# First rows of a two-layer retention block loaded tile by tile, normalised on VectorE, and transposed into two banks

## What is computed

```python
# the first stage: x = x + _L0_attn_a_ref(_layernorm(x, axis=-1), ...), where X is the argument
for i in range(L):
    Xn = _layernorm(X, ln1_w[i], ln1_b[i])
    Q = jnp.einsum('bsd,hdk->bhsk', Xn, WQ[i])
    K = jnp.einsum('bsd,hdk->bhsk', Xn, WK[i])
    V = jnp.einsum('bsd,hdk->bhsk', Xn, WV[i])
    Q = Q * cosq + _rotate_every_two(Q) * sinq
    K = K * cosk + _rotate_every_two(K) * sink
    scores = jnp.einsum('bhsk,bhtk->bhst', Q, K) * Dm[None]
    Yh = jnp.einsum('bhst,bhtk->bhsk', scores, V)
    Y = _groupnorm(Yh.transpose(0, 2, 1, 3).reshape(B, S, H * HD), gn_w[i], gn_b[i])
    G = jax.nn.silu(Xn @ WG[i])
    Y = G * Y @ WO[i] + X
    Yn = _layernorm(Y, ln2_w[i], ln2_b[i])
    X = jax.nn.silu(Yn @ ffn_w1[i] + ffn_b1[i]) @ ffn_w2[i] + ffn_b2[i] + Y
```

## Time and profile before

| | us |
|---|---|
| median of 3 runs | 1516.62 |
| lowest and highest | 1515.74, 1516.77 |
| the profiled execution | 1518.72 |
| its span, first to last instruction | 1516.9 |

### The profile page before, as it was taken

The page is one execution under the profiler, slowest core; times in us unless marked ns, Lnnn a source line. Parts: engine busy times, 40 slices in busy tenths (PEclk is TensorE's granted clock), DMA queues, the critical chain, the costliest instruction groups (busy, mean ns, idle before and its releaser), DMA issues. The chain is left out here.

```text
span 1516.9 us, 36350 instructions
## 1 busy us (share of the span) xinstructions
PE 1443.2 (95%) x13066; PEld 1196.5 (79%) x13066; DVE 1046.7 (69%) x2272; ACT 936.7 (62%) x1760; POOL 809.2 (53%) x843
## 2 busy tenths in 40 slices
PE   4999999899998999999999999997999999989998
PEld 3777777799996788887899988886777777768886
DVE  4777877565446887785755668775777777756775
ACT  5556555465554545545655567775777777757775
POOL 2566676312013666663523257775666666636674
PEclk9999999999999999999999999999999999999999
DMA  7000000100001000000300010000000000000011
GB/s 247 2 2 2 0 2 2 35 1 1 1 1 56 2 2 0 1 2 1 125 29 15 1 40 1 0 1 2 2 1 0 0 0 0 0 2 1 31 41 42
DMA packets 21095, 26.27 MB, mean 17 GB/s; under 512 B 1904, under 2 KB 19056, under 8 KB 20848
## 3 DMA queue, kind: packets, MB, share of 16 engines
q1 hardware_dynamic: 18432, 21.64, 4.3%
q10 hardware_dynamic: 2544, 3.04, 0.6%
HBM read 20.48 MB, written 4.19 MB: 16 GB/s over the span
## 5 line engine op out<-in xcount | busy, mean ns | idle before, releaser
L543 DVE TENSOR_TENSOR ffn_h_lo<-ffn_h,ffn_h_hi 128x512 fp32r<-128x512 f32 x112 | 94.0, 841 | 116.1 <-ACT ffn_h_hi L750 116.0
L749 ACT ACTIVATE ffn_h<-ffn_hp,c_b 128x512 f32<-128x512 f32 x112 | 77.2, 689 | 153.2 <-PE ffn_hp L846 152.7
L543 DVE TENSOR_TENSOR ternary_ffn_h_lo<-ternary_ffn_h,ternary_ffn_h_hi 128x512 fp32r<-128x512 f32 x128 | 110.0, 860 | 75.0 <-ACT ternary_ffn_h_hi L750 74.8
L1187 POOL TENSOR_TENSOR ret_qk<-ret_qk,ret_qk_sin 128x512 f32<-128x512 f32 x64 | 82.6, 1291 | 103.2 <-DVE ret_qk_sin L1284 102.7
L857 PE MATMUL ternary_ffn_yp<-down_ternary,ternary_ffn_h_hi 128*128 128x256 f32 x512 | 132.6, 291 | 0.0
L857 PE MATMUL ffn_yp<-down_hi,ffn_h_hi 128*128 128x256 f32 x448 | 127.7, 285 | 0.9 <-DVE ffn_h_lo L543 0.9
L857 PE MATMUL ternary_ffn_yp<-down_ternary,ternary_ffn_h_lo 128*128 128x256 f32 x512 | 127.6, 281 | 0.0
L1193 POOL TENSOR_TENSOR ret_rstd<-ret_sums,ret_minus_half 128x16 f32<-128x16 f32 x32 | 103.7, 3240 | 42.9 <-DVE ret_sums L1326 42.9
L857 PE MATMUL ffn_yp<-down_hi,ffn_h_lo 128*128 128x256 f32 x448 | 125.2, 279 | 0.0
L857 PE MATMUL ffn_yp<-down_lo,ffn_h_hi 128*128 128x256 f32 x448 | 125.2, 279 | 0.0
L2081 POOL TENSOR_TENSOR win_rms<-win_rms,win_minus_half 128x20 f32<-128x20 f32 x31 | 115.2, 3716 | 2.6
(11 more groups left out here) (315 smaller groups left out, 4786.5 us busy)
## 6 DMA issues: line engine op xcount, KB each, us to landing
X<-in_x SPq DMA_DIRECT2D x8, 512.0 KB, 10.1
staging<-in_w SPq DMA_DIRECT2D x4, 1024.0 KB, 8.5
ffn_x_in<-in_x SPq DMA_DIRECT2D x8, 512.0 KB, 3.9
out<-X SPq DMA_DIRECT2D x7, 512.0 KB, 2.9
rotary<-in_rotary ACTq DMA_DIRECT2D x1, 1024.0 KB, 7.6
staging<-in_w_up SPq DMA_DIRECT2D x1, 1024.0 KB, 4.9
staging<-in_w_down SPq DMA_DIRECT2D x1, 1024.0 KB, 7.5
staging<-in_wqkv ACTq DMA_DIRECT2D x1, 768.0 KB, 5.9
```

Source lines behind the costliest of these rows:

```text
L543: nc.vector.tensor_tensor(h_lo[:, m % R, :], h[:, m % R, :], h_hi[:, m % R, :].bitcast(F32), ALU.subtract).then_inc(h_ready, 1)
L749: nc.scalar.activation(h[:, m % R, :], hp[m % 2][:, :], fn, bias=bias)
L1187: nc.gpsimd.tensor_tensor(qk[:, r, :, :, :], qk[:, r, :, :, :], qk_sin[:, r, :, :, :], ALU.add).then_inc(qk_done, 1)
```

## The change

- SyncE loads block 0 as four tiles of 128 KB, each with its own semaphore; blocks 2 to 7 wait until the tables of ScalarE's queue have landed.
- ScalarE issues ident and ln1 first, loads its activation table, waits for tile 0, and then issues wqkv, rotary and decay, wg and wo, and the other tables.
- VectorE waits for each tile's rows by itself. For blocks 0 and 1 GpSimd makes the scale of the projections alone (`first_scale`), and VectorE normalises the rows with it (`first_normalise`); the scale of the rows in place is made later (`scale_in_place`), and ScalarE writes the rows of block 1 in place in step 2 of body 1.
- The second half of block 0 is transposed into tr[0], without a wait for the first.
- The low half of wv (2) comes after the first input_low, that of the gate (3) and the statistics of block 1 at the end of body 0, that of the output (4) behind first_normalise(1) in body 1. SyncE's wait for all five low halves ahead of in_w stays as it is.

The core of the diff (the waits, the order and the new functions; left out are the declarations of semaphores and unchanged lines around):

```diff
--- before.py
+++ after.py
+        def transposed(b, j):
+            return tr[0] if first is not None and at_start(b) and j == 1 else tr[1]
...
         @block.sync
         def _(sp):
             if first is not None:
-                for b in range(NB):
+                for t in range(TB):
+                    sp.dma_start(X[:, t, :], first["x"][P * t:P * (t + 1), :]).then_inc(tile_loaded[t], 16)
+                for b in range(1, NB):
                     at = b // 2 + CPB * (b % 2)
                     if b == 1:
                         sp.wait_ge(qkv_loaded, 16)
+                    if b == 2:
+                        sp.wait_ge(tables_loaded, 16 * (len(first["tables"]) - 2))
                     sp.dma_start(X[:, TB * at:TB * (at + 1), :],
                                  first["x"][BT * at:BT * (at + 1), :].rearrange("(t p) d -> p t d", p=P)
                                  ).then_inc(x_loaded[b], 16)
...
+            def first_scale(b):
+
+                pool.wait_ge(mv_done, b + 1)
+                apart(pool, pool_waited)
+                nc.gpsimd.tensor_scalar(work[:, 0, 0, :], mv[:, b, :, 1], 1.0 + EPS, EPS * EPS, ALU.mult, ALU.add
+                                        ).then_inc(eps_added, 1)
+                pool.wait_ge(eps_added, 2 * b + 1)
+                nc.gpsimd.tensor_tensor(scale[:, b, 0, 0, :], work[:, 0, 0, :], minus_half[:, 0:TB], ALU.pow
+                                        ).then_inc(first_scaled, 1)
+
+            def scale_in_place(b):
+
+                apart(pool, pool_waited)
+                nc.gpsimd.tensor_scalar(work[:, 0, 1, :], mv[:, b, :, 1], EPS, None, ALU.add).then_inc(eps_added, 1)
+                pool.wait_ge(eps_added, 2 * b + 2)
+                nc.gpsimd.tensor_tensor(scale[:, b, 0, 1, :], work[:, 0, 1, :], minus_half[:, 0:TB], ALU.pow
+                                        ).then_inc(scale_work, 1)
+                pool.wait_ge(scale_work, 2 * b + 1)
+                nc.gpsimd.tensor_tensor(work[:, 1, 1, :], mv[:, b, :, 0], scale[:, b, 0, 1, :], ALU.mult
+                                        ).then_inc(scale_work, 1)
+                pool.wait_ge(scale_work, 2 * b + 2)
+                apart(pool, pool_waited)
+                nc.gpsimd.tensor_scalar(scale[:, b, 1, 1, :], work[:, 1, 1, :], -1.0, None, ALU.mult
+                                        ).then_inc(scale_done, 1)
...
                     if k % TB == TB - 1 and fresh(2 * i + k // TB):
-                        scales(2 * i + k // TB, k // TB)
+                        if first is not None and at_start(i):
+                            first_scale(k // TB)
+                            if k == TB - 1:
+                                scale_in_place(0)
+                        else:
+                            scales(2 * i + k // TB, k // TB)
+                    if first is not None and at_start(n):
+                        scale_in_place(1)
...
+            def x_wait(b, at, t):
+
+                if at_start(b):
+                    dve.wait_ge(tile_loaded[t], 16)
+                elif isinstance(b, int):
...
+                if first is not None and not last_block(b) and not after_last(b) and (t == 0 or at_start(b)):
+                    x_wait(b, at, t)
...
+            def first_normalise(b):
+
+                dve.wait_ge(first_scaled, b + 1)
+                if b == 1:
+                    dve.wait_ge(tp_full, KD)
+                for t in range(TB):
+                    last = nc.vector.tensor_scalar(xn[:, t, :], X[:, CPB * TB * b + t, :], mv[:, b, t, 0:1],
+                                                   scale[:, b, 0, 0, t:t + 1],
+                                                   ALU.subtract, ALU.mult)
+                last.then_inc(xn_done, 1)
...
                     if first is not None and at_start(n):
-                        dve.wait_ge(tables_loaded, 16 * len(first["tables"]))
+                        dve.wait_ge(rotary_loaded, 16 * 2)
                     if live(n, NT):
                         rotate(n, i, k - AHEAD)
+                    if first is not None and at_start(n - 1):
+                        dve.wait_ge(tables_loaded, 16 * (len(first["tables"]) - 2))
                     if live(n - 1, NT):
                         masked(n - 1, k - 1)
                     if live(n, NT):
                         values(n, k)
+                    if first is not None and at_start(n):
+                        first_normalise(1)
+                        own_low(4)
...
+                        if first is not None and at_start(i) and k == TB + 1:
+                            own_low(2)
+                        if first is not None and at_start(i) and k == U - 1:
+                            own_low(3)
+                            for t in range(TB):
+                                statistics(1, 0, 1, t)
+                            aggregate(1, 1)
...
+                    if first is not None and at_start(i) and k >= TB:
+                        pass
+                    elif fresh(2 * i + k // TB) or (after_last(2 * i + k // TB) and i == N):
...
                     if at_start(i) and k == TB - 2:
                         if first is not None:
+                            first_normalise(0)
                             centre_values()
-                            for j in range(3):
+                            for j in range(2):
                                 own_low(j)
                         dve.wait_ge(consts_set, 3)
-                    if at_start(i) and k == TB and first is not None:
-                        for j in range(3, len(first["halves"])):
-                            own_low(j)
...
+                    last = nc.scalar.activation(out, transposed(b, j)[:, :], ACT.Identity,
...
+                        if t == 0 and fresh(b + 1) and not (first is not None and isinstance(b, int) and b < 1):
                             normalise(b + 1, i, at + 1)
-                            if first is not None and at_start(b + 1):
-                                act.wait_ge(weights_loaded, 16 * (len(first["weights"]) - 1))
-                                for j in range(3, len(first["halves"])):
-                                    own_high(j)
-                            elif first is not None and not last_block(b + 1):
+                            if first is not None and not last_block(b + 1):
                                 rows_in_place(b + 1, i, at + 1)
+                        if t == 2 and first is not None and at_start(b):
+                            act.wait_ge(scale_done, 2)
+                            rows_in_place(1, i, at + 1)
                         if live(n, NT):
                             gates(b, t // 2, at)
...
+                        if first is not None and at_start(i) and k == TB + 1:
+                            act.wait_ge(early_loaded, 16 * len(first["early"]))
                         if fresh(b + 1):
                             inputs(b + 1, t // 2, at + 1)
+                        if first is not None and at_start(i) and k == TB + 1:
+                            act.wait_ge(v_centred, 1)
+                            own_high(2)
+                        if first is not None and at_start(i) and k == U - 1:
+                            act.wait_ge(weights_loaded, 16 * (len(first["weights"]) - 1))
+                            for j in range(3, len(first["halves"])):
+                                own_high(j)
...
                         act.wait_ge(qkv_loaded, 16)
                         own_high(0)
                         own_high(1)
-                        act.wait_ge(v_centred, 1)
-                        own_high(2)
                     if at_start(i) and k == U - 1 and first is not None:
+                        act.wait_ge(scale_done, 1)
                         rows_in_place(0, i, 0)
-                        act.wait_ge(tables_loaded, 16 * len(first["tables"]))
+                        act.wait_ge(tables_loaded, 16 * (len(first["tables"]) - 2))
                     if isinstance(i, int) and i == 1 and k < len(halves):
...
             if first is not None:
+                prefetch(act, first["early"], early_loaded)
+                act.wait_ge(consts_set, 1)
+                nc.scalar.activation(table_set[:, :], minus_half[:, 0:1], ACT.Silu)
+                act.wait_ge(tile_loaded[0], 16)
                 prefetch(act, first["weights"][0:1], qkv_loaded)
-                prefetch(act, first["early"], early_loaded)
+                prefetch(act, first["tables"][0:2], rotary_loaded)
                 prefetch(act, first["weights"][1:], weights_loaded)
-                prefetch(act, first["tables"], tables_loaded)
-                act.wait_ge(early_loaded, 16 * len(first["early"]))
-                nc.scalar.activation(table_set[:, :], ident[:, 0:1], ACT.Silu)
+                prefetch(act, first["tables"][2:], tables_loaded)
...
                 if at_start(g) and first is not None:
```

(40 more changed lines are left out.)

## The result

The changed kernel is slower: 1521.38 us against 1516.78 for the one before (medians of 18 runs each), a ratio of 1.0031 with a 95% interval of 1.0025 to 1.0038, or about 4.7 us. The forecast was 1519.9, 3.3 us slower. The profiled execution has a span of 1518.9 us against 1516.9; single executions spread over 5.0 us before and 6.9 after, so the span's 2.0 us say less than the ratio, and what follows is read at points of the first 60 us.

The account below looks back on a forecast made before the run. The start was taken as bound by transferred bytes, with in_w's landing ending the last wait. The 5.1 us won are spent waiting and in_w lands 3.3 us later: median 1516.62 plus 3.3 is 1519.9 us, range 1514.5 to 1522.8.

Parts of the forecast that it names:

- What bounds the start: First 50 us: bytes bound the start, in_w landing at 29.3 behind 9.33 MB; the work chain ahead has slack.
- Start: Block 0 up to the first projection: it comes at 16.0 instead of 21.14, 5.1 us earlier.
- What moves behind it: VectorE and GpSimd work behind the first projection: own_low(4) ends at 22.9, releasing SyncE's in_w issue, before at 16.77.
- Transfers: Start-up loads: same bytes but engines stand empty at times, so in_w lands at 32.6 instead of 29.3, +3.3 us.
- the time of 1517.4 at the higher rate: Time if the last 5.24 MB of loads passed at the fabric's 435 GB/s, in 12.0 us.
- the forecast's own floor from in_w's issue: in_w alone, issued at 22.9, lands no earlier than 31.3, +2.0 us.
- A rule weighed in the forecast: Transfers from any engine share the same 16 DMA engines, so reordering can't shorten the load phase.
- Everything behind the restart as before: After in_w lands all runs as before, low clock for 5.9 us included, so the 3.3 us reach the end.
- A: Rival: the start's 5.1 us reach the end, a gain, 1511.5 us; chance 0.12.
- B: Rival: transfer gaps are filled and the rate rises towards 411 GB/s, no change, 1516.6 us; chance 0.12.
- C: Rival: own_low(4) becomes the bound and delays in_w's issue, +5.3 us, 1521.9 us; chance 0.07.
- D: Rival: ScalarE's issues keep the first projection near 21, in_w at 36.4, +7 us, 1523.7 us; chance 0.02.

Follow-up runs that it names:

- e1: Changed kernel with the eight pairs of w1/w2 halves made in steps 4 to 7 of body 1, so nothing waits for in_w at step 0: 0.9950 of before.
- e2: Kernel before the change, with the w1/w2 halves moved to steps 4 to 7 of body 1 in the same way: 0.9981 of before.
- e7: Changed kernel with own_low(4) made right behind own_low(3) at the end of body 0, the wait for the tables kept: 1.0024 of before.
- e5: Changed kernel without SyncE's wait for the tables, and own_low(4) made right behind own_low(3) at the end of body 0: 1.0009 of before.
- e8: e1 with the last eight tables issued by SyncE ahead of block 1, and no wait for the tables: 0.9957 of before.
- e12: e10 with wqkv issued by ScalarE ahead of its table load, without waiting for tile 0: 0.9964 of before.
- e4: Kernel before the change, with only SyncE's wait for the tables ahead of X block 2 added: 1.0017 of before.
- e9: e1 with both halves of block 0 transposed into one bank again: 0.9960 of before.
- e10: e1 with the last eight tables issued by SyncE behind X block 1, the wait for them kept: 0.9941 of before.
- e11: e1 with block 0 loaded by one transfer of 512 KB instead of four tiles: 0.9964 of before.

## Why the prediction was right

**What bounds the start.** Right. in_w's landing releases ScalarE, then VectorE, then TensorE; the landing and the restart both moved by 4.70 us, and e1 and e2 show no loss without that wait beyond the 0.65 us named there. How sure it was is another matter: the forecast gave 0.49 to slower and 0.39 to no change.

**Start, 16.0 predicted, 16.53 measured.** Right in its parts: tile 0 at 3.2 (3.6 predicted), normalisation ended at 8.9 (9.4), ScalarE free at 11.3 (10.6). The last is where the 0.5 us went: some of its issues took 1.0 to 1.3 us instead of 0.57, and its high halves start when its queue is through, not when wqkv lands.

**What moves behind it, own_low(4) ended at 22.9 predicted, 23.97 measured.** About half of the 1.07 us came with the first projection, 0.53 late. The other half is first_normalise(1), which took 2.23 us, not the 1.38 of the earlier trace rows; see the last section. In_w's issue at 23.99 was in time all the same, since the X blocks kept the transfer engines busy, as e7 shows.

**Transfers.** The mechanism was right, the size of one term not: the time from the last full-rate bytes of the tables to SyncE's next issue. The forecast had all 4.09 MB passed at 15.1 and the tables' semaphore at 15.7. Measured, 268 GB/s on average up to 15.1 are 4.05 MB, 99% of them. The rate was lower than taken (341 instead of 360 GB/s behind 5.4), but 0.73 MB had passed by then instead of 0.59. The last hundredth is what took long (stretches, columns as above):

```profile
14.00:15.00 1.00, 1.00 0.69 204
15.00:15.50 0.50, 1.00 0.21 73
15.50:16.00 0.50, 1.00 0.07 27
16.00:16.50 0.50, 1.00 0.05 20
```

A share of 0.07 or 0.05 is about one of the sixteen engines, as at the end of e5's transfers. SyncE issued block 2 at 16.95: 1.85 us behind 15.1 where I had put 0.6, so 1.2 us of the miss are this tail. Behind that issue 131 GB/s passed from 18.0 to 18.6, 31 until 19.0 and 381 from 19.2 on. Counted from 18.6 that is a lead of 1.7 us (1.8 taken), 14.8 us for the 5.24 MB (14.6 predicted) and 0.6 of tail. So in_w's +3.3 was mis-sized by 1.4 us. Two slips of the sum itself are smaller: 32.1 and 0.6 are 32.7, not 32.6, and the time of 1517.4 at the higher rate lies under the forecast's own floor from in_w's issue (+2.0, 1518.6).

A rule weighed in the forecast held. The Trainium skill (DMA: Bandwidth & Descriptors, Issuing engines are not separate DMA queues) has the transfers of all queues share the same engines, and e8 and e12 agree: with the tables handed to SyncE's queue ahead of block 1, wqkv on ScalarE's landed at 10.2 instead of 8.7, and with wqkv issued 1.5 us earlier the last tile on SyncE's landed 4 us later.

**Everything behind the restart as before.** Right in kind, but the low clock lasted 3.9 us instead of the 5.9 I carried over, which gave back 1 us in the profiled execution. With 4.7 at the restart the forecast would so have been 3.7 there; the ratio says 4.7, with 3.8 to 5.8 as its interval, and where that last us lies no trace shows. Whether the clock's stretch differs from run to run or belongs to the longer idle time isn't settled: e4, idle for 4.85 us, also shows a mean of 0.52 from 33 to 40 and 1.00 from 40 on.

**The rivals.** A, the gain, needed in_w's wait away: with it away (e1) it is 7.6 us, of which 2.9 are the old kernel's own wait and slow restart (e2) and 4.7 the change, near my 5.1. B's filled gaps are nearest in e5, 1.0009, whose interval takes in no change; in the changed kernel the gaps stayed open. C, own_low(4) as the bound, decides nothing that the runs can show with the tables' wait in place (e7). D falls by the first projection at 16.53, where it had 21.

## What to carry to other kernels

Before a start-up chain is shortened, ask what ends the last wait behind it: here a prefetch at the end of a full transfer queue, so that 5 us won by reordering were spent waiting, and the waits added to win them left the transfer engines short of work and cost 4.7 us on top. Move the consumer of such a prefetch first (two edits; 2.9 us for the old kernel, and the change turned from a loss of 4.7 us into a gain of 4.7 by it), then reorder the loads. A load that is needed first has to be kept alone in the queues, even if the engines run at half their rate for two us: with weights beside it the last tile of 128 KB landed 4 us later.

## What the runs showed of the hardware that I had not expected

A VectorE instruction took three times as long beside one of GpSimd. The four normalisations of block 1 took 2.23 us, those of block 0 1.39. The first of the four is the one that grew; VectorE's timeline at 21.14 and GpSimd's beside it:

```profile
21.14 1.26 DVE L1394 TENSOR_SCALAR xn<-X,mean_var,ret_scale 128x256 f32<-128x256 f32 x1
```

```profile
20.97 1.28 POOL L1222 TENSOR_TENSOR ret_qk<-ret_qk,ret_qk_sin 128x512 f32<-128x512 f32 x1 [0.64 <-DVE ret_qk_sin L1328]
```

GpSimd's sum began 0.17 us ahead and ended at 22.25; the VectorE instruction, 0.40 us by itself, ended at 22.40. GpSimd's sum was not held up: 1.28 us, against 1.26 to 1.30 at its other places. The same 2.23 or 2.24 stands in e9, e10, e11 and e12. The Trainium skill (SBUF — State Buffer, Who interferes with whom) says that VectorE in a 2-port mode and GpSimd lock a shared pair of ports, and the second to come is blocked until the first is done. This pair of instructions agrees with it. That it is the cause isn't shown: no run shows the mode that the instruction ran in, and the next normalisations, from 22.32 on, took 0.40 us each although GpSimd's power (22.65, 1.03 us) ran beside them. The slow one cost 0.85 us in block 1. On ScalarE, idle for 3.99 us at that point, the four take 2.07 us, little less than the 2.23 here, but VectorE would have been free for own_low(4); no run here has them there.

Transfers issued one behind the other on one queue don't land one by one. wqkv, 768 KB issued at 3.17, landed 6.4 us later in the changed kernel, with rotary's 1 MB issued 0.4 us behind it; by 9 us that queue had moved 1.59 MB, twice what wqkv holds, and wqkv landed at 9.57.
